# An eighth embedding table picked by one-hot products, and a finer order of VectorE's work

## What is computed

```python
e = jnp.stack([tbl_0[ids[:, 0]], ..., tbl_25[ids[:, 25]]], axis=1)    # 512 x 26 x 128
sd = jnp.einsum('bfd,bd->bf', e, dense)                              # dots with the dense features
ss = jnp.einsum('bfd,bgd->bfg', e, e)                                # dots of all pairs of rows
z = concatenate([dense, sd, ss[upper triangle]], axis=1)
h = concatenate([z, dense], axis=1)                                  # 607 numbers
h = maximum(h @ W_top1 + b_top1, 0)                                  # 512
h = maximum(h @ W_top2 + b_top2, 0)                                  # 256
y = h @ W_top3
```

## Time and profile before

| | us |
|---|---|
| median of 3 runs | 119.27 |
| the runs | 117.73, 119.27, 120.22 |
| profiled execution | 118.29 |
| its span | 115.5 |
| outside the span | 2.8 |
| PE, weight load, VectorE, ScalarE, GpSimd busy | 102.7, 88.9, 63.5, 58.6, 77.0 |

### The profile page before, as it was taken

The page is one execution under the profiler, slowest core; times in us unless marked ns, Lnnn a source line. Parts: engine busy times, 40 slices in busy tenths (PEclk is TensorE's granted clock), DMA queues, the critical chain, the costliest instruction groups (busy, mean ns, idle before and its releaser), DMA issues.

```text
span 115.5 us, 1946 instructions
## 1 busy us (share of the span) xinstructions
PE 102.7 (89%) x696; PEld 88.9 (77%) x696; DVE 63.5 (55%) x140; ACT 58.6 (51%) x133; POOL 77.0 (67%) x88
## 2 busy tenths in 40 slices
PE   0789999999999598999999999398998999789991
PEld 0365867668687486999998998297988999679981
DVE  4789999999999933277653223215150243162030
ACT  4399899589949932445592427404302213261110
POOL 3777677877777776777777677677777777442000
PEclk9999999999999999999999999958999999999999
DMA  2998564616789421222232232112223212101000
GB/s 46 284 268 218 187 182 108 200 47 198 160 240 372 161 60 45 53 61 52 58 104 69 67 86 75 45 48 64 54 64 101 61 45 71 48 3 40 9 0 1
DMA packets 5709, 11.71 MB, mean 101 GB/s; under 512 B 2600, under 2 KB 3070, under 8 KB 5701
## 3 DMA queue, kind: packets, MB, share of 16 engines
q1 hardware_dynamic: 3141, 6.55, 19.4%
q0 software_dynamic: 2560, 5.05, 17.2%
HBM read 10.86 MB, written 0.00 MB: 94 GB/s over the span
## 4 chain that ended last, share of the span: by engine, by line
POOL 46%; PE 31%; issue 15%; DMA 4%; ACT 1%; DVE 1%
POOL rows L320 46%; PE ps_gram L405 11%; PE ps_h_bank L433 7%; DMA rows<-in_cold,cold_rows 2%; PE ps_dve L446 2%; PE ps_h_bank L461 2%; PE ps_dve L382 2%; PE ps_h_bank L418 2%; DMA cold_ids_sb<-in_cold_ids 2%; PE ps_h_bank L473 1%; PE ps_act L382 1%; PE ps_h_bank L464 1%; PE ps_h_bank L456 1%; ACT h L806 1%; DVE vecs L585 1%
## 5 line engine op out<-in xcount | busy, mean ns | idle before, releaser
L320 POOL DMA_INDIRECT rows<-in_cold,cold_rows x72 | 70.0, 973 | 21.9 <-issue 21.3
L405 PE MATMUL ps_gram<-vecs 128*122 128x108 f32 x256 | 31.7, 279 | 1.6 <-DVE vecs L585 0.9
L405 PEld LDWEIGHTS ps_gram<-vecs 128*122 128x122 f32 x256 | 30.2, 195 | 2.5 <-ACT vecs L730 1.6
L348 PE MATMUL ps_gram<-one_hot,table_hi 125*128 125x512 f32 x58 | 23.8, 430 | 1.3 <-issue 1.3
L597 DVE TENSOR_TENSOR one_hot<-ps_gram,row_id 125x1024 fp32r<-125x1024 f32 (+1 forms) x22 | 24.0, 1140 | 0.7 <-PE ps_h_bank L339 0.7
L348 PE MATMUL ps_gram<-one_hot,table_lo 125*128 125x512 f32 x58 | 22.6, 410 | 0.0
L348 PEld LDWEIGHTS ps_gram<-one_hot,table_hi 125*128 125x128 f32 x58 | 10.9, 197 | 5.9 <-issue 3.3
L585 DVE COPY vecs<-ps_dve 128x128 f32<-128x128 f32 (+2 forms) x20 | 8.1, 438 | 10.0 <-PE ps_dve L382 9.9
L348 PEld LDWEIGHTS ps_gram<-one_hot,table_lo 125*128 125x128 f32 x58 | 11.2, 196 | 2.9 <-DVE table_lo L609 0.6
L793 ACT COPY sums_even<-ps_gram 26x216 f32<-26x216 f32 (+1 forms) x20 | 5.9, 296 | 13.8 <-PE ps_gram L405 13.7
L641 DVE COPY sums_even<-ps_gram 26x216 f32<-26x216 f32 (+1 forms) x20 | 6.5, 327 | 11.5 <-PE ps_gram L405 11.3
(11 more groups left out here) (63 smaller groups left out, 95.4 us busy)
## 6 DMA issues: line engine op xcount, KB each, us to landing
table<-in_tbl SPq DMA_DIRECT2D x6, 448.0 KB
rows<-in_cold,cold_rows POOLq DMA_INDIRECT x72, 2.5
w_dots<-in_w_dots SPq DMA_DIRECT2D x1, 768.0 KB, 5.4
table<-in_tbl SPq DMA_DIRECT2D x1, 560.0 KB
w_dense<-in_w_dense SPq DMA_DIRECT2D x1, 512.0 KB, 4.9
w<-in_W_top SPq DMA_DIRECT2D x1, 512.0 KB, 8.7
table<-in_tbl SPq DMA_DIRECT2D x6, 52.0 KB
dense<-in_r_dense_features SPq DMA_DIRECT2D x1, 256.0 KB, 3.7
```

What stands on the lines that cost most here:

```text
L320: pool.indirect_dma_start(out=rows[:, t % ROW_SETS, n, :], out_offset=None, in_=ins["cold"], in_offset=bass.IndirectOffsetOnAxis(ap=(cold_ ...
L348: return pe.matmul(ps_pick[:, i % 2, :], part[0:KP, (STEP_AT[i] + k) % PART_STEPS, :], one_hot[0:KP, (STEP_AT[i] + k) % HOT_STEPS, :], sta ...
L405: last = pe.matmul(ps_gram[0:TAKEN, b0 + (g - g0) // PER_BANK, c0:c0 + COLS], vecs[:, t % 2, p0:p0 + QUADS, :].rearrange("d p f -> d (p f) ...
```

## The change

`HOT` gets an eighth table (number 3, 1250 rows, ten steps), and the picked tables are put in another order: the two of ten steps are now third and sixth. So there are 68 steps instead of 58, and 18 gathers a tile instead of 19, two of them for tables beyond 16 (`EXTRA_WIDTHS`). ScalarE makes three steps in tables 1, 3, 5 and 7 and two in the others.

VectorE no longer makes a table's low parts in one go. A piece of two steps is made behind each pair of one-hots (`low_part(i, piece)`), with a count of its own in `s_lo`. PE waits for the piece that it needs, and SP, before it loads into a ring place, for the last piece of the table there (`PIECES_TO`). The copies that stood behind a table's low parts now stand behind its second pair. Group 4 of tile 0 is read inside table 7, ahead of its last one-hot, where it was read behind the loop. PE's order has pick(7) behind the transpose of group 6.

```diff
--- before.py
+++ after.py
@@ -21,7 +21,7 @@
 TABLE_ROWS = [125000, 12500, 1250, 1250, 12500, 1000, 1000, 1000, 1250, 12500, 12500, 1250, 12500,
               12500, 1250, 12500, 1000, 1250, 12500, 1000, 1250, 1250, 1250, 1250, 1000, 1250]
 
-HOT = [5, 6, 7, 16, 19, 24, 2]
+HOT = [5, 6, 2, 7, 16, 3, 19, 24]
 NHOT = len(HOT)
 KP = 125
 KP_A = 112
@@ -30,10 +30,13 @@
 STEP_COUNTS = sorted(set(KTS))
 ROW_ID_AT = [sum(n for n in STEP_COUNTS if n < kt) for kt in KTS]
 
-KS_ACT = [[4, 5, 6] if i in (1, 2, NHOT - 1) else [4, 5] for i in range(NHOT)]
+KS_ACT = [[4, 5, 6] if i in (1, 3, 5, 7) else [4, 5] for i in range(NHOT)]
 RUNS_DVE = [[(0, 2), (2, 4)] + [(k, min(k + 2, KTS[i])) for k in range(max(KS_ACT[i]) + 1, KTS[i], 2)]
             for i in range(NHOT)]
 STEP_AT = [sum(KTS[:i]) for i in range(NHOT)]
+
+PIECE = 2
+PIECES_TO = [sum(KTS[:i]) // PIECE for i in range(NHOT + 1)]
 HOT_STEPS, PART_STEPS, TABLE_RING = 24, 20, 3
 EARLY = 1 + NHOT
 
@@ -47,8 +50,7 @@
 
 JOINED = COLD[MAIN:] + COLD[:MAIN]
 JOINED_AT = {f: sum(TABLE_ROWS[g] for g in JOINED[:k]) for k, f in enumerate(JOINED)}
-EXTRA_WIDTHS = [w for w in (1, 2, 4) if (len(COLD) - MAIN) & w]
-assert EXTRA_WIDTHS[0] == 1
+EXTRA_WIDTHS = [1, 1]
 EXTRA_AT = [MAIN + sum(EXTRA_WIDTHS[:n]) for n in range(len(EXTRA_WIDTHS))]
 GATHERS = [(EXTRA_AT[n], w, p) for n, w in enumerate(EXTRA_WIDTHS) for p in range(0, P, P // w)]
 GATHERS += [(0, MAIN, p) for p in range(0, P, P // MAIN)]
@@ -259,7 +261,7 @@
             def load_table(i):
                 whole = ins[f"tbl_{HOT[i]}"].rearrange("(p k) d -> p k d", k=KTS[i])
                 if i >= TABLE_RING:
-                    sp.wait_ge(s_lo, i - TABLE_RING + 1)
+                    sp.wait_ge(s_lo, PIECES_TO[i - TABLE_RING + 1])
                 sp.dma_start(table[0:KP_A, i % TABLE_RING, 0:KTS[i]], whole[0:KP_A]).then_inc(s_table[i], 16)
                 sp.dma_start(table[KP_A:KP, i % TABLE_RING, 0:KTS[i]], whole[KP_A:KP]).then_inc(s_table[i], 16)
 
@@ -358,11 +360,13 @@
                         if k == k0:
                             pe.wait_ge(s_hot_dve, steps_made(RUNS_DVE, i, n + 1))
                     products(k, table_hi)
+                    if k == 0:
+                        continue
+                    if k == 1 or k % PIECE == 0:
+                        pe.wait_ge(s_lo, PIECES_TO[i] + k // PIECE + 1)
                     if k == 1:
-                        pe.wait_ge(s_lo, i + 1)
                         products(0, table_lo)
-                    if k >= 1:
-                        last = products(k, table_lo)
+                    last = products(k, table_lo)
                 last.then_inc(s_picked, 1)
 
             def transposes(t, g):
@@ -501,6 +505,7 @@
             transposes(0, 5)
             pick(6)
             transposes(0, 6)
+            pick(7)
             transposes(1, 0)
             pe.wait_ge(s_pad, 2)
             pe.wait_ge(s_dense_read, 2)
@@ -599,20 +604,20 @@
                     row_id[0:KP, at + k0:at + k1].unsqueeze(2).to_broadcast(shape), ALU.is_equal
                     ).then_inc(s_hot_dve, 1)
 
-            def low_part(i):
-
-                dve.wait_ge(s_hi, i + 1)
-
-                for k0, k1, m in part_runs(i):
-                    for k in range(k0, k1, 2):
-                        n = m + k - k0
-                        last = nc.vector.tensor_sub(table_lo[0:KP, n:n + 2], table[0:KP, i % TABLE_RING, k:k + 2],
-                                                    table_hi[0:KP, n:n + 2].bitcast(F32))
-                last.then_inc(s_lo, 1)
+            def low_part(i, piece):
+
+                if piece == 0:
+                    dve.wait_ge(s_hi, i + 1)
+                k, n = piece * PIECE, (STEP_AT[i] + piece * PIECE) % PART_STEPS
+                nc.vector.tensor_sub(table_lo[0:KP, n:n + PIECE], table[0:KP, i % TABLE_RING, k:k + PIECE],
+                                     table_hi[0:KP, n:n + PIECE].bitcast(F32)).then_inc(s_lo, 1)
 
             for i in range(NHOT):
+
                 one_hots(i, 0)
-                low_part(i)
+                low_part(i, 0)
+                one_hots(i, 1)
+                low_part(i, 1)
                 if i == 2:
                     dve.wait_ge(s_dense_tp, 1)
                     nc.vector.tensor_copy(dense_t[:, :, :], ps_dve[:, :, :]).then_inc(s_dense_read, 1)
@@ -620,8 +625,12 @@
                     read_transposed(0, 0)
                 if i == 5:
                     read_transposed(0, 2)
-                for n in range(1, len(RUNS_DVE[i])):
+                if i == 7:
+                    read_transposed(0, 4)
+                low_part(i, 2)
+                for n in range(2, len(RUNS_DVE[i])):
                     one_hots(i, n)
+                    low_part(i, n + 1)
                 if i == 2:
                     dve.wait_ge(s_dense_read, 1)
                     nc.vector.tensor_copy(
@@ -629,7 +638,6 @@
                     dense_t[:, 0:DIRECT, :].rearrange("d t (h s g) -> d (t h) s g", s=QUADS, g=PER_PART))
                     nc.vector.tensor_copy(early[:, 0, :].rearrange("d (t p) -> d t p", p=P), dense_t[:, DIRECT:TILES, :]
                                           ).then_inc(s_dense_read, 1)
-            read_transposed(0, 4)
             read_transposed(0, 6)
             read_transposed(1, 0)
 
```

## The result

The changed kernel is slower: 123.78 us in the median of four runs (122.2 to 125.48) against 118.5 for the kernel before beside it, a ratio of 1.0489 (95% interval 1.035 to 1.0627). The profiled execution took 122.2 us with a span of 120.3. The forecast was 120.5 in a range of 117.7 to 122.9, and the change within 2%.

A forecast was written before the change was run, and what follows sets the result against it. PE was taken as the bound, with gathers binding at one place. Terms +5.4 - 1.8 - 1.7 - 0.2 = +1.7 us gave 120.0 by the profiled run and 121.0 by the median; 120.5 us was taken, range 117.7 to 122.9.

The forecast's parts named there:

- Direction and bound: Whole kernel: gathers bind only at one place, for 1.77 us; PE sets the rest; change within 2%, chance 0.65.
- GpSimd's rival: Whole kernel: POOL's gathers are the bound, four fewer save 5.0 us and hide the added products, 113.3 us; chance 0.05.
- Part 1, the wait: Tile 3's fifth group: with four gathers fewer, PE's 1.77 us wait for gathered rows goes, -1.8 us.
- Part 1, the clock: Behind that wait, 70 to 80 us: PE's half clock goes with the wait, -1.7 us.
- the rest: From the first Gram product to the last layer's last product: forecast 3.7 us shorter.
- Part 2, PE's added work: Picking stage: 20 products at 0.232 us and one more spreading of ids, less four transposes overall, +5.2 us.
- the stage: From the first transposes of rows to the first Gram product: forecast +5.4 us, stalls included.
- Part 3, the stalls: Picking stage: VectorE's 5.7 us more work stalls PE 0.6, 0.2 and 0.6 us; the old 1.49 us stall goes.
- The walk: Picking stage: step-by-step timing of VectorE and PE, placing PE stalls at the third and sixth tables and group 6's transpose.
- The rival of a clock that falls elsewhere: End of the picking stage: PE's idling drops it to 1.2 GHz, costing 1.7 us, 121.7 or 122.7 us; chance 0.20.
- The sum: Whole kernel: +5.4 - 1.8 - 1.7 - 0.2 = +1.7 us, span from 115.5 to 117.2 us.

The follow-up runs named there:

- f1: The kernel before, with PE's four transposes of the dense features moved behind pick(0): 119.82 us, ratio 1.0279.
- e6: The kernel before, with the third part of tile 2's Gram products ahead of that tile's group 4 transposes: 118.4 us, ratio 1.0128.
- f4: The kernel before, with half of the last tile's dense products put between the strips' products of few rows: 120.52 us, ratio 1.0179.
- e1: The kernel before (seven tables, 19 gathers a tile), with only VectorE's new order of low parts in pieces: 118.29 us against 117.68, ratio 1.012.
- g5: The kernel before, with 4 identity products ahead of the first spreading and 2 behind the second: 118.2 us, ratio 1.0136.
- e2: The kernel before with 18 gathers a tile, the last gathered table left out and seven tables still picked: 118.69 us against 117.68.
- e3: The changed kernel, with each table's low parts made in one go behind its first pair of one-hots: 125.61 us, ratio 1.0736.
- e5: The changed kernel, with VectorE's group 4 read ahead of the eighth table's one-hots and ScalarE's group 1 and 3 reads behind its own: 121.57 us, ratio 1.0416.
- g1: e5's kernel, with ScalarE making three steps in every table but the third: 122.28 us, ratio 1.0511.
- g2: The changed kernel, with ScalarE making two steps in every table: 123.66 us, ratio 1.0624.
- f2: e5's kernel, with PE's dense transposes moved behind pick(0): 122.15 us in the median of four, against 117.66 for the kernel before.
- e4: The changed kernel, with VectorE reading group 4 of tile 0 ahead of the eighth table's one-hots: 121.88 us, ratio 1.0406.
- e8: The changed kernel, with products of the identity by itself added at PE's start: 123.54 us against 123.78.
- e7: The kernel before, with 8 identity products ahead of the first spreading and 3 behind the second: 117.72 us, ratio 1.0058.

## Why the prediction was wrong

**Direction and bound: right in part.** "The gathers bind at one place, for 1.77 us, and PE is the engine that sets the rest" held: GpSimd's rival (113.3 us) is dead, and the four gathers bought next to nothing: without its fall f1 (19 gathers, first Gram product at 48.3) takes 65.7 us from there to the end, as the changed kernel does.

**Part 1, the wait: mis-sized.** "The 1.77 us go" took no account of what that wait covered, ScalarE's read of group 3, 0.76 us in the profile after. The strips' landing is waited for 0.5 longer as well. That leaves 0.5. And in runs that reach tile 2 later there was no wait to remove (e6, f1, f4), so it is not the gathers that took it away.

**Part 1, the clock: the step that failed.** "If that is the cause, another 1.46 + 0.28 go" took one execution's fall for the wait's doing. e1 and g5 have longer waits and no fall behind them; e2, e3, e5, g1 and g2 (18 gathers) and f1 (19) have no wait for rows, and all have a fall at the end. Of the kernel before's 47 runs beside the experiments 27 had a mean clock below 0.99, of the changed kernel's five with a clock on record three. So nothing shows that the change takes falls away, and the 1.7 us can't be counted as its gain; what brings a fall stays open. Between the two profiled executions they appear all the same, by luck: the one before had its fall, at 75 us, and the one after had none. The 2.3 us by which the rest was shorter hold them, and 0.5 is left without. What the rule of the Trainium skill cited there (TensorE: Matmul & The Clock Gate, "HAM oscillation — how this bites in real kernels") says of waits for a DMA had one row for it and has e1's against it, for a wait of this length; the page's own example has longer ones.

**Part 2, PE's added work: right.** 4.64 + 0.87 - 0.18 = 5.3 us without stalls, with 1.0 at the end, gives 30.9 for the stage; e5 took 31.34 with 0.29 of waiting, f2 30.82. The products came 0.233 apart, as the row said, and not the 131 ns of the Trainium skill (TensorE: Matmul & The Clock Gate, "Back-to-back issue gap").

**Part 3, the stalls: mis-sized, and one link missed.** The walk put 0.6 + 0.2 + 0.6 on PE; the trace has 0.62 + 0.67 + 0.81 and 0.44 more. I had looked at ScalarE's one-hots and evictions near the end, and had not walked its list. Its read of group 1 waits for a PE that is a ten-step table later than before, its rounding comes late, VectorE loses 0.89 us, and PE 0.5 of that at the sixth table; the fifth table's start waits, by its list, for ScalarE's evicting (done at 30.49). e5 beside e4 shows this chain: moving ScalarE's two reads takes about 1.0 of the 6.64 us back, and e4's move of VectorE's read another 0.92. The rival of a clock that falls elsewhere had the price (1.6 us), but neither the place nor the cause.

**The sum.** On the profiled executions: start +0.4 (forecast 0), stage +6.6 (+5.4), rest -2.3 (-3.7), in all +4.7 to the last product, against +1.7. The profiled executions themselves are 3.9 apart, as 1.9 us lie outside the span after and 2.8 before. On the medians it is 5.3: the profiled execution after had no fall of the clock while three of its other four runs had, and the one before had one (3.9 + 1.7 = 5.6). The range ended at 122.9, 0.9 short.

## What to carry to other kernels

Where three engines are level, a table more on one of them must be walked through all three lists, with every read that stands ahead of other work in one list and waits for another engine: such reads turned a cost of about 4.7 us into 6.6. What a wait had covered has to be priced before the wait is counted as gain. And a fall of the clock in one execution is no term of a sum until several executions have it at the same place.

## What the runs showed that was not expected

- The stage between two fixed events differs by 0.2 us in the eight profiles with seven tables (26.73 to 26.91), while the spans of the kernel before spread over 6 us. The spread is in the start and in the clock. With eight tables the stage is less fixed: PE then waits for VectorE in it, and less so when the start made PE late (0.62 at the third table in the profile after, 0.29 in e5, nothing in f2).
- PE starts at 1.2 GHz (0.43 us for 512 columns) and comes to 2.4 GHz (0.23) between 10 and 13 us in some profiles, between 15 and 17 in others, which puts the first Gram product of seven tables at 45 or at 48. With identity products ahead it is there at 5.5 us, in one profile for good (e8), in the other until 8 us (e7). The granted clock in the profile shows this only in e7.
- A fall to half clock came with no gap ahead of it, at the products behind those of few rows, and cost 1.6 us (e2, from 108 to 112 us). What brings it stays open.
- What the times of e1 have against its profile (1.2% and none) stays open too; no run was made for it.
